# A recommendation tower on one core: dot products two samples at a time in wider matmuls, layers in the dots' PSUM banks, and gathers of a group issued in one row

## The reference

```python
e = jnp.stack([tbl_0[ids[:, 0]], ..., tbl_25[ids[:, 25]]], axis=1)      # (2048, 26, 128)
combined = jnp.concatenate([dense_features[:, None, :], e], axis=1)     # (2048, 27, 128)
interactions = jnp.einsum('bnd,bmd->bnm', combined, combined)
interactions_flat = interactions[:, _TRIU_I, _TRIU_J]                   # 351 pairs
h = jnp.concatenate([dense, interactions_flat, dense], axis=1)          # 607 numbers
h = jnp.maximum(h @ W_top1 + b_top1, 0.0)                               # 512
h = jnp.maximum(h @ W_top2 + b_top2, 0.0)                               # 256
y = h @ W_top3                                                          # (2048, 1)
```

## Time and profile before

| | |
|---|---|
| median of 3 runs | 597.74 us (596.02 to 600.65) |
| the profiled execution: time, span from first to last instruction | 598.93 us, 597.2 us |
| TensorE busy, its weight loads | 466.2 us (78%), 423.9 us (71%) |
| DVE, ACT, GpSimd busy | 256.7 us (43%), 176.1 us (29%), 296.0 us (50%) |
| mean granted clock of TensorE | 0.842 of full |
| moved by DMA | 28.02 MB, 47 GB/s in the mean |

### The profile page before, as it was taken

How to read it: one execution, slowest core, us unless ns; L and a number is a source line. 1 busy time by engine, 2 the same in 40 slices (tenths; PEclk the granted TensorE clock), 3 DMA queues, 4 the chain that set the end, 5 groups by cost and what they waited for, 6 DMA issues and landing times.

```text
span 597.2 us, 14574 instructions
## 1 busy us (share of the span) xinstructions
PE 466.2 (78%) x6057; PEld 423.9 (71%) x6057; DVE 256.7 (43%) x465; ACT 176.1 (29%) x443; POOL 296.0 (50%) x314
## 2 busy tenths in 40 slices
PE   3564677697988889676997979688797969977787
PEld 1463666586977878576886868677686858877776
DVE  3853458251544446252452626344262623622340
ACT  1231233332324332132322314132232423224341
POOL 7777144554554455455554545555554554545200
PEclk9557689897878988888888979869797796988899
DMA  5453211111111111111111111111111111111000
GB/s 116 157 171 88 73 27 39 38 44 37 36 45 35 42 37 46 38 38 42 36 46 33 46 33 44 38 35 42 41 45 37 33 45 32 41 37 38 23 3 1
DMA packets 19577, 28.02 MB, mean 47 GB/s; under 512 B 10691, under 2 KB 13267, under 8 KB 19518
## 3 DMA queue, kind: packets, MB, share of 16 engines
q0 software_dynamic: 9728, 19.94, 12.7%
q1 hardware_dynamic: 9790, 7.17, 4.1%
HBM read 27.08 MB, written 0.01 MB: 45 GB/s over the span
## 4 chain that ended last, share of the span: by engine, by line
PE 71%; issue 15%; ACT 3%; DMA 3%; another core or an unknown queue 3%; DVE 3%; SPq 1%; DVEq 0%; ACTq 0%
PE dots_ps L394 27%; PE fetch_ps L419 22%; PE h_ps L466 9%; PE vec_ps L372 6%; PE h_ps L482 4%; DMA vecs<-in_tbl 3%; PE ids_ps L401 2%; ACT vecs L607 1%; PE fetch_ps L466 1%; DVE onehot L739 1%; ACT inter L643 1%; DVE inter L818 1%; DVE vecs L590 1%; ACT vecs L590 0%
## 5 line engine op out<-in xcount | busy, mean ns | idle before, releaser
L333 POOL DMA_INDIRECT rows<-in_tbl,idx x304 | 293.5, 965 | 262.5 <-DMA rows<-in_tbl,idx 154.4
L394 PE MATMUL dots_ps<-vecs 128*27 128x27 f32 x4096 | 162.3, 202 | 73.1 <-issue 71.6
L394 PEld LDWEIGHTS dots_ps<-vecs 128*27 128x27 f32 x4096 | 148.1, 118 | 88.4 <-issue 85.8
L419 PE MATMUL fetch_ps<-onehot,t_hi 125*128 125x256 f32 x448 | 136.0, 327 | 38.4 <-ACT vecs L607 24.7
L818 DVE COPY_PREDICATED inter<-mask,dots_ps 27x128 f32<-27x128 int32 (+2 forms) x256 | 66.7, 260 | 205.4 <-ACT inter L643 198.9
L739 DVE TENSOR_TENSOR onehot<-ids_ps,row_of 125x1024 fp32r<-125x1024 f32 x94 | 111.2, 1220 | 59.5 <-PE ids_ps L401 32.6
L419 PE MATMUL fetch_ps<-onehot,t_lo 125*128 125x256 f32 x448 | 133.5, 326 | 0.0
L419 PEld LDWEIGHTS fetch_ps<-onehot,t_hi 125*128 125x128 f32 x448 | 99.6, 222 | 43.0 <-issue 36.6
L643 ACT COPY inter<-dots_ps 27x128 f32<-27x128 f32 (+1 forms) x256 | 63.8, 249 | 179.9 <-PE dots_ps L394 106.1
L419 PEld LDWEIGHTS fetch_ps<-onehot,t_lo 125*128 125x128 f32 x448 | 100.0, 223 | 4.5 <-issue 0.2
L607 ACT COPY vecs<-fetch_ps 128x256 f32<-128x256 f32 x56 | 37.6, 672 | 125.8 <-PE fetch_ps L419 99.4
(11 more groups left out here) (65 smaller groups left out, 194.5 us busy)
## 6 DMA issues: line engine op xcount, KB each, us to landing
rows<-in_tbl,idx POOLq DMA_INDIRECT x304
vecs<-in_tbl SPq DMA_DIRECT2D x6, 500.0 KB
rows<-in_r_dense_features SPq DMA_DIRECT2D x16, 64.0 KB
h_sb<-in_W_top_laid SPq DMA_DIRECT2D x2, 512.0 KB
w_sb<-in_W_top SPq DMA_DIRECT2D x1, 512.0 KB
w_sb<-in_tbl SPq DMA_DIRECT2D x1, 500.0 KB
idx<-in_ids SPq DMA_DIRECT2D x16, 13.0 KB
w_dense<-in_W_top SPq DMA_DIRECT2D x1, 256.0 KB
```

Source lines behind the costliest of these rows:

```text
L333: nc.gpsimd.indirect_dma_start(out=rows[v % 2][:, s, :], out_offset=None, in_=tables[f - 1][:, :], in_offset=bass.IndirectOffsetOnAxis(ap= ...
L394: last = pe.matmul(dots_ps[q * 32:q * 32 + N, n // HALF, o:o + N], vs[:, b, :], vs[:, b, :], start=True, stop=True)
L419: last = pe.matmul(fetch_ps[:, 0:R], part[0:KP, k, h * KH + t, :], onehot[buf][h][0:KP, t, :], start=(h == 0 and t == 0 and part is t_hi), ...
```

## The change

The program is changed in these points:

- `vecs` has 32 columns a sample (`NP`) where it had 27, the last five zero. A matmul of `dots` takes two samples: the stationary operand is 2 x 32 columns, the moving one 2 x 27, the output 64 x 54, of which the two diagonal blocks are used. There are 64 for a tile in two halves, and `dots_ps` has four banks; `dots_done` counts halves.
- Layer 1 writes to the four banks of `dots_ps` in one piece per block of 128 outputs, after the merge of the dots before has ended; the next dots wait until it is rectified. Layers 2 and 3 write there as well. Layer 3 yields one row of 256 numbers.
- `AT_ONCE` is 4, and no group has more, so that no gather waits for a landing. The second group waits for the first half of the dots instead of the first quarter.
- The order of lookups, layers and transposes around the dots is another one. `in_first_tile` issues a lookup after the second and after the fourth group of an even tile's transposes, `in_second_tile` a block of layer 1 after each of the second to fifth group of an odd tile's.
- The ids of the seven tables come as a further input with an id's samples in a row, and are no longer turned by TensorE. The tables are loaded in pieces of 112 and 13 partitions. The output is written from one partition. The scratch for the descriptors of the gathers is set to 2048 bytes a partition.

```diff
-AT_ONCE = 2
+AT_ONCE = 4
...
-        vecs = [sb(f"vecs{s}", [P, 2, P, N]) for s in range(2)]
+        vecs = [sb(f"vecs{s}", [P, 2, P, NP]) for s in range(2)]
...
-        dots_ps = ps("dots_ps", [P, 2, 512])
-        h1_ps = ps("h1_ps", [P, M1 // 2, R])
-        h2_ps = ps("h2_ps", [P, M2, R])
+        dots_ps = ps("dots_ps", [P, BANKS, 512])
...
-                for b in range(P):
-                    q, n = b // QS, b % QS
-                    o = (n % HALF) * N
-                    last = pe.matmul(dots_ps[q * 32:q * 32 + N, n // HALF, o:o + N], vs[:, b, :],
-                                     vs[:, b, :], start=True, stop=True)
-                    if n == QS - 1:
-                        last.then_inc(dots_done, 1)
+                    dots_banks_free(i, v - 1)
+                if not (first and v < 2):
+                    if v % 2:
+                        pe.wait_ge(relu1_done, i * (2 * M1) + v // 2 * M1)
+                    elif not (first and v == 2):
+                        pe.wait_ge(y_kept, i * 2 + v // 2 - 1)
+                for h in range(2):
+                    for n in range(QS):
+                        o = n % SLOTS * PAIR
+                        b = h * 64 + n * 2
+                        last = pe.matmul(dots_ps[h * 64:h * 64 + 64, n // SLOTS, o:o + PAIR],
+                                         vs[:, b:b + 2, :].rearrange("p b f -> p (b f)"), vs[:, b:b + 2, 0:N],
+                                         start=True, stop=True)
+                    last.then_inc(dots_done, 1)
...
+                transpose_rows(i, v, in_first_tile)
+                dots(i, v)
+                fetch_items(i, r, [2] if prev else [0])
+                transpose_rows(i, v + 1, in_second_tile)
+                fetch_items(i, r, [3])
+                dots(i, v + 1)
+                fetch_items(i, r, [4, 5])
+                if prev:
+                    layer2(*prev, False, lambda: dots_banks_free(i, v + 1))
+                fetch_items(i, r, [6])
+                if prev:
+                    layer3(*prev, False)
...
+def h1_at(m):
+    return dots_ps[:, m, 0:R]
+def dots_banks_free(i, v):
+    pe.wait_ge(inter_by_act, i * (4 * NA) + (v + 1) * NA)
+    pe.wait_ge(inter_by_dve, i * (4 * ND) + (v + 1) * ND)
...
-    nc = bacc.Bacc("TRN2", target_bir_lowering=False, num_devices=1)
+    nc = bacc.Bacc("TRN2", target_bir_lowering=False, num_devices=1, dynamic_dma_scratch_size=2048)
```

More of the change, by code:

```diff
@@ L355, in _, with transpose_rows @@
         def _(pe):
-            def transpose_rows(i, v, ks=range(NG), after=lambda k: None):
+            def transpose_rows(i, v, after=lambda k: None):
                 u = v % 2
-                for k in ks:
-                    group = groups[k]
+                for k, group in enumerate(groups):
                     kk = v * NG + k
@@ L435, in layer1 @@
-            def layer1(i, r, half, some=range(L1)):
-                spare = isinstance(i, int) and i == PASSES - 1
+                    fetch(k, *item(i, r, k), i * 2 + r + 1)
+            def layer1(i, r, ms, free):
                 tiles = i * 4 + (r + 1) * 2
-                bank = h1_half(half, spare)
-                for n in some:
-                    m, at = divmod(n, 3 * (JG + 1))
-                    c0 = (half * (M1 // 2) + m) * P
-                    if n == 0 and half == first_half(i, r):
+                for m in ms:
+                    if m == 0:
@@ L487, in layer3 @@
[L487 to L497 removed]
+                        free()
@@ new lines, in layer1 @@
+                    for at in range(3 * (JG + 1)):
+                        if at < 2 * (JG + 1):
+                            jj, w, x = at // 2, (w_hi, w_lo)[at % 2], x_hi
+                        else:
+                            jj, w, x = at - 2 * (JG + 1), w_hi, x_lo
+                        last = pe.matmul(h1_at(m), w[:, jj, m * P:(m + 1) * P], x[:, jj, :],
+                                         start=(at == 0), stop=(at == 3 * (JG + 1) - 1))
+                    last.then_inc(h1_done, 1)
@@ new lines, in layer2 @@
+            def layer2(i, r, spare, free=lambda: None):
+                pe.wait_ge(mlp_w_in, 64)
+                pe.wait_ge(relu1_done, i * (2 * M1) + (r + 1) * M1)
+                free()
+                for m in range(M2):
+                    for k in range(M1):
+                        last = pe.matmul(h2_at(m, spare), w2_sb[:, k, m * P:(m + 1) * P], h1_sb[:, k, :],
+                                         start=(k == 0), stop=(k == M1 - 1))
+                    last.then_inc(h2_done, 1)
```

560 lines of the change are left out of this document (239 added, 321 removed).

## The result

The changed kernel takes **682.4 us** (median of 4 runs, 673.0 to 683.6) where the kernel before takes 596.9 us (593.2 to 600.7): ratio 1.135, 95% interval 1.117 to 1.152. Single runs of one kernel scatter by up to 3%, and the ratios compare the faster ones of each kernel; the two medians alone would give 1.143. I had forecast 546 us, and 606 as the upper end of the range. The profiled execution took 683.3 us for a span of 681.5.

The account below looks back on a forecast made before the run. TensorE was taken as the bound, starved of instructions beside gathers, with GpSimd hardly slack. Span 597.2 - 66.5 (dots) + 21.7 (banks) - 8 (start) + 1 (end) = 545.4 us, forecast 546 us, range 488 to 606.

Parts of the forecast that it names:

- Fewer, longer dots: Dot products at L394: 128 matmuls of 54 columns a tile for 256 of 27, less starvation, 66.5 us less.
- the share of slow matmuls: Dots beside gathers: same share of half as many matmuls, 13 slow, each 0.23 us longer: 3.0 us, 11.0 a tile.
- the lost silences: GpSimd loses the pauses in which TensorE recovered; up to three groups, 15 us, can follow each other.
- Layers in the dots' banks: Layer 1 and the next dots wait for each other's banks: 3.1 us a round, 7 rounds, +21.7 us.
- the four waits that I named: Per round: layer 1 behind the merge 0.4 us, even dots 0.9, second of two lookups 0.8, first comparison 1.0.
- Gathers without the landing wait: GpSimd issues each group in one go, needing 23.75 us a tile instead of 35, so it is off the bound.
- neither half of this change could give much alone: GpSimd's two tiles take 70.5 us, TensorE's 70.9, so dots or gathers changed singly gain little.
- Start: Up to the first dots: ids need no transposes, tables land earlier; 59 us for 67.4, -8 us.
- Scratch: Gather descriptor scratch cut to 2048 bytes: no cost in the sum; rival of GpSimd waiting for room, 575 to 595 us, 5%.
- Unbroken gathers did starve TensorE: Rival: long rows of gathers starve dots, lookups and layer 1 of instructions; 616 us, 16%.
- The gaps are not a matter of the number of instructions: Rival: gathers stop TensorE 45% of the time whatever it does, dots 14.5 us a tile; 603 us, 12%.
- Starvation vanishes: Rival: the new dots' instruction demand stays under what comes, no starvation left; 493 to 504 us, 22%.

Follow-up runs that it names:

- without gathers: Gathers of tiles 2 to 15 left out, their transposes using the rows that lie there: 453.1 us for the kernel before, 548.9 us for the changed one.
- With pauses: Changed kernel with two gathers in a row, then two GpSimd selects as a pause in place of the landing wait: 597.3 us.
- the other half alone: Kernel before with AT_ONCE = 4, gathers of a group four in a row and no wait for landing: 640.5 us, ratio 1.079.
- the last chip: Last batch's chip: changed kernel, compare between merges and fifth lookup's copy before the split: 498.2 us with rows of four, 513.7 with one-select pause; kernel before 585.2.
- the two moves: Changed kernel, sixth lookup's compare between merges and fifth lookup's copy ahead of the split: 523.1 us without gathers of tiles 2 to 15, 574.3 with two-select pauses.

## Why the prediction was wrong

The three parts of the loss, from runs in which "remote" waits show (the changed kernel with rows of two is 612.2, without gathers 548.9 us):

| step | worked out | us |
|---|---|---|
| changed order, banks, start, no gathers | 548.9 - 453.1 | +96 |
| what gathers in rows of two cost, now less before | (612.2 - 548.9) - (596.5 - 453.1) | -80 |
| rows of four instead of two | 682.4 - 612.2 | +70 |
| sum | 682.4 - 596.5 = 86 | +86 |

By the lowest run of each instead of the median the three are +99, -77 and +63, so none is known to better than some 7 us.

Against the forecast the loss is best laid out by the spans of the profiled executions. "Dots" is the time from the first to the last matmul of each tile, summed; waits ahead of a tile's first matmul (1.7 us in all before) fall under "all else".

| part of the span | before | forecast | measured | off by |
|---|---|---|---|---|
| dots of 16 tiles | 233.7 | 168.9 | 181.3 | +12 |
| start, up to the first dots | 67.4 | 59.4 | 76.6 | +17 |
| all else, without gathers beside it | 266.6 | +22.7 | 351.8, +85.2 | +63 |
| all else, what gathers add to it | 29.5 | as before | 71.8, +42.3 | +42 |

Two steps failed: the price of the shared banks and the new order (63 us), and what gathers add outside the dots, which the sum had at nothing (42 us, and the start's 17 beside them). That this is mostly late signals follows from the chain, where "another core or an unknown queue" holds 109 us.

**Fewer, longer dots: mechanism right, size nearly.** "Streaming itself thus gains almost nothing; the gain must come from starvation" held: 127.1 us for 114.8 without gathers, 153.8 for 235.4 with rows of two, 81.6 us less where I had 66.5. With rows of four it is 211.7, but 30.4 of it are waits ahead of the tiles' first matmuls (before 1.7, without gathers 7.5), most of which go with the late signals. At 157.35, for instance, TensorE's wait of 5.17 us is put down to "issue", while ACT's copy of the last transposes, which the dots need, had begun only at 156.41, "remote". The matmuls themselves took 181.3 us for my 168.9. With pauses they took 154.6, so 27 us are the price of the longer rows, of which I counted a part: I held the share of slow matmuls fixed and left the lost silences out of the sum.

**Layers in the dots' banks: the step that failed most.** I priced new waits at 3.1 us a round, +21.7 us, bounds 0 and about twice. Taking the span less dots and start, the two kernels without gathers need 443.1 - 113.1 - 63.4 = 266.6 and 548.0 - 119.6 - 76.6 = 351.8 us: **+85 us**. Of the four waits that I named two stand in every round about as priced: 0.9 us ahead of even dots, 1.1 ahead of layer 1 (I had 0.4 to 0.8); a third, the copy between two lookups (0.8), shows as 0.98 once the longer wait there is gone; the fourth (1.0) I didn't find by itself. What I missed was the order inside VectorE's and ScalarE's queues. I asked what each TensorE instruction waits for, not what stands in front of its releaser: the sixth lookup's comparison and the fifth's copy behind all merges (4.9 us a round and the clock behind it; 26 us outside dots and start, shown by moving both). Another 15 us came with the wider matmul in the old order and banks (281.6 for 266.6). I also costed the new strides at nothing, since DVE is idle half the time; a merge takes 366 ns for 260, 3.4 us a round, and sits on the path from dots to layer 1 now that both share banks. If these parts add up, some 45 of the 85 us remain, in the rounds 4.3 us each (54.8 against 50.5). That the strides are part of it is argued, not tested.

**Gathers without the landing wait.** I had GpSimd freed and a loss only through TensorE's instruction supply. The freeing was right: no landing waits, and with them the merged dots were bound by GpSimd (612.2), as "neither half of this change could give much alone" had it. That the other half alone gave nothing either (640.5) is no support: it lost 44 us to something that I hadn't counted. The loss came mostly by another road, late signals to ACT and DVE: against the kernel with pauses, rows of four cost 59 us outside dots and start (423.6 for 364.6) and 27 in them. The trace of before showed the kind of wait twice. The 9.95 us of "another core or an unknown queue" stand beside the longest row of gathers in that kernel; I noted that its cause had no name. And in its rounds ACT's copies of the dots waited 68.9 us for "remote", up to 5.7 us at a time, which I didn't look up. I priced neither in the rounds, where the change was to make rows longer.

**Start:** -8 forecast, +9.2 measured (first dots at 76.6). The table lookups were early as I had it, and then two pauses of 11.2 and 20.3 us, for 9.95 and two short ones before, stood in the chain beside the row of 38. **Scratch:** nothing, as taken.

**The rivals.** Unbroken gathers did starve TensorE, but its threshold, dots of 14.7 us a tile, was never reached (211.7 / 16 = 13.2, or 11.3 without the waits ahead of them) while the kernel still became slower: the price lay in signals and order. Its 616 us was nearest of all, for another reason than it gave. "The gaps are not a matter of the number of instructions" falls by 81.6 us. "Starvation vanishes" is what the last chip shows. Its 498 us lies within that rival's 493 to 504 by luck: it has the two moves, and a start 9 us earlier than I had. The Trainium skill (Runtime: NRT & Kernel Launch, Instruction fetch mechanics) holds that fetch is hidden; by that rule no dots should have gaps with "issue" from it. The last chip's trace agrees (7.5 us idle, none of it "issue"), and so do those without gathers; the traces with gathers on the others don't (17.7 to 77.4 us), if these gaps are fetch, which no view names.

## What to carry to other kernels

When instructions move to shared banks or coarser steps, walk each helper engine's queue in order and ask what each release stands behind. When one such wait is removed, the next queue may hold the same one, so move both before judging. Run both kernels once without the suspected disturber: two such runs split this result into parts that the full traces had mixed. Look up in the trace what an edit meant to space out really does: "two in a row" were mostly four here. And an unexplained wait in the trace of before is a price to carry into the forecast, above all if the change makes its surroundings more common.

## What the hardware showed

- While GpSimd issued rows of gathers, signals between other engines came late: waits up to 23.1 us in the changed kernel and 29.6 us in another beside 38 in a row. The end of such a wait came 4.6 us after the row of 38 (60.29 against 55.69, changed kernel without later gathers) and 1.15 us after a row of four in the round shown. That it is the signal that is late is inferred; no view names the cause.
- Gaps of 1.7 us (596.3 to 575.4) or 1.2 us (595.1 to 575.9) in a group, in place of landing waits of 2.3 us and more, won 3% in the kernel before. In the changed kernel gaps of 1.2 to 1.3 us went with 635.4 us and gaps of 1.7 with 597.3.
- This disturbance isn't always there: the same copy waited 22.4 us for "remote" on one chip and 3.9 us for its own matmuls on another, and there a round beside 38 gathers was as long as one without (54.78 and 54.77 us).
- A 27 x 27 matmul with its weight load took 27 ns and one of 64 x 54 took 58 ns back to back, so merging two samples gains nothing by itself at full clock.
